# A sigmoid recurrence over 3600 tokens: sixteen images in one chain, or eight and eight in two

## The reference

```python
def _L1_ffn_ref(x, W, V, gamma, beta):
    Wx = jnp.einsum('bti,hi->bth', x, W)             # all tokens at once
    ...                                              # batch norm of Wx over images and tokens, gamma, beta
    Vt = V.T
    def step(yt, wx_t):
        yt = jax.nn.sigmoid(wx_t + yt @ Vt)
        return (yt, yt)
    _, ys = jax.lax.scan(step, y0, jnp.swapaxes(Wx, 0, 1))
    return jnp.swapaxes(ys, 0, 1)
...
t = t + _L1_ffn_ref(_ln_t(t), ...)
```

## Time and profile before

| | |
|---|---|
| median of three runs | 4467.57 us |
| the profiled execution, its time | 4466.31 us |
| its span, first to last instruction | 4464.5 us |
| PE (TensorE) busy | 4333.0 us, 97% |
| PEld (its weight loads) busy | 2749.2 us, 62% |
| ACT (ScalarE) busy | 1472.4 us, 33% |
| DVE (VectorE) busy | 1330.0 us, 30% |
| POOL (GpSimd) busy | 101.2 us, 2% |
| mean granted clock of TensorE | 0.979 |

### The profile page before, as it was taken

How to read it: one execution, slowest core, us unless ns; L and a number is a source line. 1 busy time by engine, 2 the same in 40 slices (tenths; PEclk the granted TensorE clock), 3 DMA queues, 4 the chain that set the end, 5 groups by cost and what they waited for, 6 DMA issues and landing times.

```text
span 4464.5 us, 106022 instructions
## 1 busy us (share of the span) xinstructions
PE 4333.0 (97%) x42695; PEld 2749.2 (62%) x42695; DVE 1330.0 (30%) x2487; ACT 1472.4 (33%) x5370; POOL 101.2 (2%) x163
## 2 busy tenths in 40 slices
PE   7999999998899999999999899999999999999999
PEld 2899999984463799999993333333333333333333
DVE  3655533335535655533335500000000000000000
ACT  5002344445534102344443133333333333333333
POOL 1000000000000000000000000000000000000000
PEclk9999999999978999999999999999999999999999
DMA  5000000013237100000006200000000000000000
GB/s 139 11 0 0 0 0 0 0 30 104 86 92 221 44 0 0 0 0 0 0 0 187 68 14 18 18 9 18 18 18 18 9 18 18 18 9 18 18 18 13
DMA packets 146727, 139.17 MB, mean 31 GB/s; under 512 B 79550, under 2 KB 146142, under 8 KB 146654
## 3 DMA queue, kind: packets, MB, share of 16 engines
q1 hardware_dynamic: 146654, 138.21, 12.0%
HBM read 79.18 MB, written 58.98 MB: 31 GB/s over the span
## 4 chain that ended last, share of the span: by engine, by line
PE 94%; DVE 3%; ACT 1%; issue 1%; DMA 0%; POOL 0%; SPq 0%; DVEq 0%; ACTq 0%; POOLq 0%; PEldq 0%
PE ps L790 22%; PE ps L725 20%; PE ps L703 17%; PE ps L871 16%; PE ps L785 3%; PE ps L531 3%; PE ps L552 3%; PE ps L542 2%; PE ps L591 1%; PE ps L523 1%; PE ps L676 1%; DVE rstd L1112 1%; PE ps L643 1%; PE ps L581 1%; PE ps L818 1%
## 5 line engine op out<-in xcount | busy, mean ns | idle before, releaser
L790 PE MATMUL ps<-idle 128*32 128x512 bf16 (+1 forms) x5894 | 1633.3, 339 | 0.8 <-DVE xl L1091 0.8
L871 PEld LDWEIGHTS ps<-xl,vt 65*32 65x32 f32 x14400 | 521.2, 108 | 1163.5 <-ACT xl L1084 1111.3
L1084 ACT ACTIVATE xl<-ps 64x16 f32<-64x16 f32 x3600 | 637.2, 177 | 1252.1 <-PE ps L871 1252.1
L725 PE MATMUL ps<-xl,taps 128*128 128x128 f32 (+2 forms) x7880 | 913.9, 279 | 4.8 <-DVE xl L1284 4.8
L725 PEld LDWEIGHTS ps<-xl,taps 128*128 128x128 f32 x7880 | 913.6, 191 | 5.4 <-issue 5.4
L871 PE MATMUL ps<-xl,vt 65*32 65x16 f32 x14400 | 871.4, 193 | 7.9
L703 PE MATMUL ps<-split 128*128 128x400 f32 x4140 | 780.2, 351 | 13.3 <-DVE split L1279 13.3
L703 PEld LDWEIGHTS ps<-split 128*128 128x128 f32 x4140 | 778.2, 190 | 16.5 <-issue 15.1
L1352 DVE TENSOR_TENSOR xl<-xl 64x480 f32<-64x480 f32 x120 | 116.5, 971 | 1774.2 <-PEq L868 888.0
L941 ACT ACTIVATE img<-xl 128x144 f32 x788 | 366.8, 465 | 548.0 <-DVE xl L1261 548.0
L1261 DVE SCALAR_TENSOR_TENSOR xl<-ps,img 128x144 f32<-128x144 f32 x788 | 323.9, 411 | 589.0 <-PE ps L725 589.0
(11 more groups left out here) (141 smaller groups left out, 1720.6 us busy)
## 6 DMA issues: line engine op xcount, KB each, us to landing
ring<-in_x_dram SPq DMA_DIRECT2D x144, 200.0 KB, 3.6
x_dram<-sums SPq DMA_DIRECT2D x144, 200.0 KB, 3.4
t_dram<-sums SPq DMA_DIRECT2D x72, 200.0 KB, 3.6
ring<-t_dram SPq DMA_DIRECT2D x72, 200.0 KB, 3.8
ring<-x_dram SPq DMA_DIRECT2D x72, 200.0 KB, 3.7
xl<-x_dram SPq DMA_DIRECT2D x30, 480.0 KB, 6.2
out_dram<-xl SPq DMA_DIRECT2D x30, 480.0 KB, 4.7
img<-in_L_ffn_weight_dram SPq DMA_DIRECT2D x4, 512.0 KB
```

Of the source, the lines that this page charges most:

```text
L725: last = pe.matmul(acc[:, :, lo:hi], taps[:, (k * NO + d + 2) * 128:(k * NO + d + 3) * 128], column[h][:, :, lo + d:hi + d], start=(n == 0 ...
L790: pe.matmul(PS[bank][0:32, 0:n], idle[:, 0:32], idle[:, 0:n], start=True, stop=True)
L871: last = pe.matmul(PS[s][c * 32:(c + 1) * 32, t * B:(t + 1) * B], vt[:, c * 32:(c + 1) * 32], prev, start=False, stop=True, skip_group_che ...
L1084: act.activation(yb[0:64, s % 2, :, t], PS[s % 2][0:64, t * B:(t + 1) * B], ACT.Sigmoid).then_inc(step_y, 1)
```

## The change

The sixteen images become two chains of eight. In every step TensorE issues the product of images 0 to 7, then either a part of the fill or a keeping matmul, then the product of images 8 to 15, then a keeping matmul. Each chain has its own PSUM banks (`ps0` and `ps2` for the first, `ps1` and `ps3` for the second), its own `step_mm` and `step_y`, and its own sigmoid of 64 by 8. The keeping matmuls all have 256 columns now and write to `ps4`. A segment has 20 steps, so there are 180 segments where there were 120, the fill has 8 parts, and a unit of loading and storing is 80 tokens (45 of them).

```diff
-SEG = 30
+SEG = 20
...
-            acc = PS[j][0:64, 0:SEG * B].rearrange("p (t b) -> p t b", b=B)
+            acc = PS[2 * j + h][0:64, 0:SEG * HB].rearrange("p (t b) -> p t b", b=HB)
             for c in range(2):
-                last = pe.matmul(acc[c * 32:(c + 1) * 32, t0:t0 + FILL_T, h * HB:(h + 1) * HB], wsc[h][:, c * 32:(c + 1) * 32],
-                                 stage[j][:, t0:t0 + FILL_T, :], start=(part == 0), stop=True, skip_group_check=True)
+                last = pe.matmul(acc[c * 32:(c + 1) * 32, t0:t0 + FILL_T, :], wsc[h][:, c * 32:(c + 1) * 32],
+                                 stage[j][:, t0:t0 + FILL_T, :], start=(t0 == 0), stop=True, skip_group_check=True)
...
-                        if n == 0:
-                            pe.wait_ge(step_y, 2 * SEG)
-                            pe.sem_clear(step_y)
-                        else:
-                            pe.wait_ge(step_y, n)
-                        if t == 0:
-                            pe.sem_inc(seg_done, 1)
...
-                        if t < 2 * FILLS:
-                            if t == 0:
-                                pe.wait_ge(staged, i * 2 + (s + 2))
-                            last = fill_input(pe, 1 - s, t)
-                            if t == 2 * FILLS - 1:
-                                last.then_inc(filled, 1)
-                            keep_clock(pe, 512)
-                        else:
-                            keep_clock(pe, 512)
-                            keep_clock(pe, 256)
+                        for h in range(2):
+                            if n == 0:
+                                pe.wait_ge(step_y[h], 2 * SEG)
+                                pe.sem_clear(step_y[h])
+                            else:
+                                pe.wait_ge(step_y[h], n)
+                            if t == 0 and h == 1:
+                                pe.sem_inc(seg_done, 1)
+                            images = slice(h * HB, (h + 1) * HB)
+                            prev = yb[:, s, images, t - 1] if t else yb[:, 1 - s, images, SEG - 1]
+                            for c in range(2):
+                                last = pe.matmul(PS[2 * s + h][c * 32:(c + 1) * 32, t * HB:(t + 1) * HB], vt[:, c * 32:(c + 1) * 32],
+                                                 prev, start=False, stop=True, skip_group_check=True)
+                            last.then_inc(step_mm[h], 1)
+                            if h == 0 and t < 2 * FILLS:
+                                if t == 0:
+                                    pe.wait_ge(staged, i * 2 + (s + 2))
+                                last = fill_input(pe, 1 - s, t)
+                                if t == 2 * FILLS - 1:
+                                    last.then_inc(filled, 1)
+                            else:
+                                keep_clock(pe, 256, 4)
...
-                        act.wait_ge(step_mm, n + 1)
-                        if n == BODY * SEG - 1:
-                            act.sem_clear(step_mm)
-                        act.activation(yb[0:64, s % 2, :, t], PS[s % 2][0:64, t * B:(t + 1) * B], ACT.Sigmoid).then_inc(step_y, 1)
+                        for h in range(2):
+                            act.wait_ge(step_mm[h], n + 1)
+                            if n == BODY * SEG - 1:
+                                act.sem_clear(step_mm[h])
+                            act.activation(yb[0:64, s % 2, h * HB:(h + 1) * HB, t], PS[s % 2 * 2 + h][0:64, t * HB:(t + 1) * HB], ACT.Sigmoid
+                                           ).then_inc(step_y[h], 1)
```

More of the change, by code:

```diff
@@ L114, in metaformer @@
         yb = xl[0:65, 0:2 * SEG * B].rearrange("p (s t b) -> p s b t", s=2, b=B)
-        x2b = xl[0:64, 1920:3840].rearrange("p (b t) -> p b t", b=B)
-        ob = xl[0:64, 3840:5760].rearrange("p (b t) -> p b t", b=B)
+        x2b = xl[0:64, 1920:1920 + BODY * SEG * B].rearrange("p (b t) -> p b t", b=B)
+        ob = xl[0:64, 3840:3840 + BODY * SEG * B].rearrange("p (b t) -> p b t", b=B)
         wsc = [xl[:, 5760 + h * 64:5824 + h * 64] for h in range(2)]
@@ L194, in metaformer @@
         passed = sem("passed")
-        step_mm, step_y, seg_done, x2_in, added, out_st = (
-            sem(n) for n in ("step_mm", "step_y", "seg_done", "x2_in", "added", "out_st"))
+        step_mm, step_y = ([sem(f"{n}{h}") for h in range(2)] for n in ("step_mm", "step_y"))
+        seg_done, x2_in, added, out_st = (sem(n) for n in ("seg_done", "x2_in", "added", "out_st"))
         staged, filled = sem("staged"), sem("filled")
@@ L873, in _ @@
-                        last.then_inc(step_mm, 1)
-                        if t < 2 * FILLS:
-                            if t == 0:
-                                pe.wait_ge(staged, i * 2 + (s + 2))
-                            last = fill_input(pe, 1 - s, t)
-                            if t == 2 * FILLS - 1:
-                                last.then_inc(filled, 1)
-                            keep_clock(pe, 512)
-                        else:
-                            keep_clock(pe, 512)
-                            keep_clock(pe, 256)
@@ L1339, in _ @@
             link(dve.memset(yb[64:65], 1.0), 8)
-            dve.memset(yb[0:64, 1, :, SEG - 1], 0.0).then_inc(step_y, 2 * SEG)
+            for h in range(2):
+                dve.memset(yb[0:64, 1, h * HB:(h + 1) * HB, SEG - 1], 0.0).then_inc(step_y[h], 2 * SEG)
             dve.wait_ge(bn_pe, 3)
```

## The result

The changed kernel takes 4436.8 us (median of four, 4434.93 to 4441.4); the kernel before, beside it, 4469.51 (4464.61 to 4477.49). The ratio to the kernel before is 0.9927, 95% interval 0.9909 to 0.9944. The forecast was 4840 us, in a range of 4430 to 4960; the time is that of rival A, 4439 us, to which I had given 0.30. It lies inside the range only because I had stretched the range to take in A; the likeliest case's own range, 4690 to 5030, misses it by 253 us. The sum at full clock was right to 2 us, and the forecast fell with its assumption on the clock.

The account below looks back on a forecast made before the run. The prediction took the recurrence to be bound by latency between product and sigmoid; at clock 0.50, 2218 us of steps plus 45 of starts make 2263 against 1890.70, +372 on 4466.3, about 4840 us, range 4430 to 4960.

Parts of the forecast that it names:

- rival A: Recurrence at full clock with the chains side by side: whole kernel 4439 us (4425 to 4455), chance 0.30.
- the likeliest case: Clock stays at 0.50 for the whole recurrence: around 4840 us, own range 4690 to 5030, chance 0.48.
- The sum at full clock: Whole kernel if the clock is 1.00: 4466.31 - 47 + 20 = 4439 us.
- The order of things: Recurrence: a latency chain of product and sigmoid, 0.52 us a step; splitting the batch alone gains nothing.
- The narrower operations: Product and sigmoid with eight columns fewer: 13 ns less a step, 47 us less over 3600 steps.
- The starts of segments: 180 segment starts instead of 120, and a second semaphore to clear: +20 us taken, +10 to +35 allowed.
- rival C: Full clock, gain eaten by 0.30 us a segment (+35) and chains displacing each other (+36): 4490 or 4472 us; chance 0.10.
- The two chains in each other's way: Queued work on TensorE and ScalarE at full clock fits within a step: 0 us taken, bounds 0 to 0.03 a step.
- The clock: TensorE's thinner stream likelier than not never gets full clock in the recurrence: +372 us.
- The row from 45.70 us: Profile window cited on the clock: TensorE busy 12.23 of 12.30 us, yet at 0.50, in matmuls with weight-load pauses.
- The price at clock 0.50: Recurrence step at 0.50: 0.565 us with a fill, 0.65 without, mean 0.616; 2263 us with starts.
- B: Full clock that doesn't hold, 30 to 60% of steps at 0.50: 4560 to 4680 us, chance 0.12.

Follow-up runs that it names:

- the one chain of 8: Kernel before with product and sigmoid of images 0 to 7 alone, other eight left out, segments of 30: recurrence 1838.5 us, device time 4425.85 us.
- as the one chain shows: Kernel before, one chain of sixteen images, with segments of 20 steps instead of 30: recurrence 1896.5 us against 1886.5, device time 4474.38 us.
- the three versions at 2027 us: Changed kernel with keeping matmuls of 128 columns, none, or 256 only behind the second product: 4607.97, 4605.66 and 4608.42 us.

## Why the prediction was wrong

*The order of things, right.* The chain bounds the step before and after, and two chains give nothing of themselves: the one chain of 8 has the step of the two, 0.505 us.

*The narrower operations, right.* 13 ns a step taken, 13.4 found; 47 us forecast, 48.0 measured.

*The starts of segments, right in sum.* I took +20 for more starts and the second semaphore. By the recurrences, less what the low clock costs in them, the starts take 38 us where they took 20: +18. Of this 10.0 are the segments of 20, as the one chain shows; the rest is that a start costs 0.21 us with two chains and not 0.17. So rival C's 0.30 a start didn't come.

*The two chains in each other's way: taken as 0, bounds 0 to 0.03 us.* It is 4.2 us in 3600 steps, 0.001 us a step, and nearly all of it lies at the starts, in the item above. In the steps themselves 0 was right.

*The clock, wrong, and this alone made the forecast.* The step that failed is "I therefore take it as likelier than not that the clock isn't granted at the start; and as these steps repeat for 1.9 ms without a denser stretch, it then isn't granted at all". What I took from the rows stands: being busy is not enough, and a thinner stream does lose the clock for good (the three versions at 2027 us, the one with 128 columns busy for 2011 of them). But the rows before held no recurrence with a thinner stream than the kernel's own, and I put the changed kernel on the wrong side of a boundary of which they showed nothing. The row from 45.70 us, on which I leaned for it, also ended too early. Of the pauses for weight loads that I named there the trace shows this much: the two passes of a matmul of 400 columns start 0.80 to 0.83 us apart with weights of 128 columns (line 531, 48.94 and 49.77 us), 0.73 with 64 (line 676, 47.40 and 48.12) and 0.67 with 32 (line 523, 52.11 and 52.78). The same lines of the kernel run on behind it, and there the clock does rise, at 62.8 us (us, busy us, PEclk, DMA share, GB/s):

```profile
58.00:62.80 4.80, 4.80 (x23) 0.50 0.49 126
62.80:66.00 3.20, 3.20 (x24) 1.00 0.31 81
```

So that stream was no case of a clock that isn't granted, only of one that is granted late. The runs put it on the right side: with its 256 columns the clock rises and all but holds; with one of the two keeping matmuls left out of the steps without a fill it is gone. I counted the columns that the change takes from the keeping matmuls and gave no weight to the product being cut in two. The kernel before with the same keeping columns has its clock down for a fifth of the recurrence, the changed kernel for 1% of it. Between them are twice the product's passes and weight loads and a step shorter by 13 ns; which of these makes the difference the runs don't tell.

*The price at clock 0.50, too dear as well.* I had 0.565 us with a fill and 0.65 without. The changed kernel's own first steps tell:

```profile
2578.01 0.30 PE L873 MATMUL ps<-xl,vt 65*32 65x8 f32 x4
2578.17 0.37 PE L790 MATMUL ps<-idle 128*32 128x256 bf16 x1
2578.31 0.30 PE L873 MATMUL ps<-xl,vt 65*32 65x8 f32 x4
2578.46 0.37 PE L790 MATMUL ps<-idle 128*32 128x256 bf16 x1
2578.60 0.30 PE L873 MATMUL ps<-xl,vt 65*32 65x8 f32 x4
```

From 2578.01 to 2578.60 is one step without a fill: 0.588 us by the sigmoids, 0.294 for a product and its keeping matmul; with a fill it is 0.553. Both lie below the bounds that I had set, 0.60 and 0.555. The product takes 0.08 beside the 0.213 of the columns, not the 0.12 that I got by halving a remainder. My sums put the products, the fill and the columns one behind the other on one path; that was my estimate, and no run shows it. What the kernel before shows at 0.50 is a keeping matmul of 512 columns that starts at 2573.53, the state ready at 2573.81, and the product's four records starting 0.33, 0.41, 0.42 and 0.49 us behind the keeping matmul, three of them before the 0.427 of its columns are over. What the changed kernel shows in the sums' place is the 0.553 and 0.588. (The prediction's lower mean of 0.575 us a step doesn't follow from these bounds, which give 0.582.) At 0.50 throughout, the recurrence would have been 3600 x (0.4 x 0.553 + 0.6 x 0.588) and the starts, 180 x 0.2: 2102 us, and the kernel about 4680 (an estimate from these steps), not 4840. So even with the clock lost the figure would have been 160 us off.

*The rivals.* A came out. B, a clock that rises and falls, is what the kernel before does with thinned columns, at 4501. That TensorE is kept from long idling doesn't decide between them: in the version with 128 columns it is busy for 2011 of 2027 us and the clock stays at 0.50.

## What to carry to other kernels

Splitting the batch into chains beside each other didn't shorten this recurrence, which is bound by latency: one chain of 8 takes 0.505 us a step and so do two. What it gave is what narrower operations save on each link, 13 ns of 519, and it had its own starts and semaphores to pay. Before a gain of 1% is built on a full TensorE clock, try the keeping work at half and at double: here the whole gain of 33 us hung on one matmul of 256 columns in the steps without a fill, whose absence costs 170 us. And a better version was one constant away: with segments of 30 the two chains take 4428.67 us, 0.9901 of the kernel before, while segments of 45 or 60 cost more than the whole gain because the loop's body has grown.

## What I had not expected of the hardware

- The return to the start of TensorE's loop lies within the 0.32 us of a segment's start with a body of 40 steps (the changed kernel), costs no more with 60, and takes about 4 us with 90 or 120, in two of the three versions with a second stall behind it. The DMA queue of the instructions, silent with the short bodies once the loop has run once, then works through the whole recurrence (327 to 345 packets from 2600 to 4400 us, against 2 with 60 steps and none with 40).
- With the clock at 0.50 the chain's step is 0.553 us whether there are no keeping columns, 128 behind each product or 256 behind one. The halved clock costs this chain only 48 ns of 505. The product's records take 0.28 us where they took 0.23, and the sigmoid stays at 170 to 171 ns.
- A stall of 4 us costs twice: at 90 of the 97 returns the clock goes down to 0.50 before the next sigmoid, and it comes back mostly 13.7 to 20.5 us later.
